# Expert layer: first product as three terms on half-height tiles, rectify and weight in one VectorE step, norm work per tile on ScalarE

## The chip, the cores and the metric

The kernel runs on one core of a Trainium2 chip. The core has a matrix engine (TensorE, PE in the profile), VectorE (DVE), ScalarE (ACT), GpSimd (POOL), and SyncE (SP), which here only issues DMAs. Matrix products land in PSUM, which is eight banks of 512 float32 values in each of 128 partitions; everything else lives in SBUF. The metric is the device time of one execution in microseconds, median of the runs.

## The reference, cut to what matters

Five layers over 8 sequences of 1,024 tokens with 64 features: a token front end, a two-layer recurrence, a routed feed-forward layer, an attention-like layer with phases, and a layer of eight experts. The change is to the last:

```python
gate_logits = x_flat @ Wg + bg + bias
topk_vals, topk_idx = jax.lax.top_k(gate_logits, TOP_K)        # TOP_K = 2 of 8
topk_w = jax.nn.softmax(topk_vals, axis=-1)
combine = (jax.nn.one_hot(topk_idx, NUM_EXPERTS) * topk_w[..., None]).sum(axis=1)
h = jax.nn.relu(jnp.einsum('td,edh->teh', x_flat, W1) + b1)    # D=64 -> 128 hidden, 8 experts
y = jnp.einsum('teh,ehd->ted', h, W2) + b2
out = jnp.einsum('ted,te->td', y, combine)
```

Its input is the layer norm of the running sum `h`, and its output is added to `h`.

## The kernel before

One program, written out by hand for each engine, with semaphores between the engines; nothing is scheduled by a planner. Stages in order: constants and lead-in (to about 45 us), the recurrence (to about 850 us, TensorE without a pause), the routed feed-forward and the phases (to about 905 us), attention (to about 985 us), and the experts (the last 145 us).

**The expert stage** runs over 64 slots, n = 8 b + e for sequence b and expert e. Every slot has this path:

- `hidden(n)` on TensorE (L1667): the first product. The normalised input of a token is kept as two float16 parts, high and low, one above the other in 128 rows of `xt`; the weights `wx[0]` and `wx[1]` (high and low) stand twice above each other. Four matmuls, of 128 rows, 128 columns and 512 tokens, fill two PSUM banks: `bank01` for even slots, `bank45` for odd ones.
- `relu(n)` on ScalarE (L1277): scale, bias and rectify from PSUM to one of eight SBUF buffers, `expert_at(n)`.
- `mult(n)` on VectorE (L2132): multiplies these by `wide[:, e, :]`, the gate weight of expert e for each token, the same in all partitions.
- `second(n)` on TensorE (L1707): the second product in float32, two matmuls of 64 columns each, one for each half of the sequence. In slot e = 0 the products of the gate weights with `eb2` (the second biases, L1718) go ahead of it.

TensorE takes the slots in pairs (L1765): for the pair (n, n + 1) it issues the first products of n + 2 and n + 3, then gate work if it is due, then the second products of n - 1 and n, then transposes. The first product of n + 2 goes into the bank of slot n, so it waits until that has been read: `pe.wait_ge(s_r, n - 1)`, a semaphore that `relu` counts up.

**Beside it, for the next sequences**, each at a fixed slot (`y, step = divmod(n + 3, NE)`):

- The norm of sequence y + 2 (`third_*`): mean, centring, variance, scaling and the low part on VectorE, squares and high part on ScalarE, the root on GpSimd, 8 transposes on TensorE (L321), a copy to `xt` on ScalarE (L327). `mean_back` adds back, on VectorE, a mean that the residual `res` is short of.
- The gates of sequence y + 1: `gates` on TensorE (step 1), `gate_logits` (step 2), `gate_greater` (4), `gate_rank` (5) and `gate_weights` (6) on VectorE, then `weights_turned` on TensorE (step 7: one transpose, L1665, issued behind the two first products of its pair), a copy on ScalarE, a DMA to DRAM and eight DMAs of 512 KB which spread the rows over all partitions (`wide`). SP issues these in order; the one for expert e waits for `mult` of expert e of the sequence before.

Of the kernel before, what the change touches and what calls it, by code (L numbers as in the profile page):

```python
# [15 lines left out]
P = 128  # L16
KEEP = 511
B, T = 8, 1024
D = 64
# [15 lines left out]
W_FF1, W_KQ1, W_V, W_G, W_E1, W_WR, W_END = W_AT = 0, 256, 384, 448, 456, 1480, 1481  # L35
# [5 lines left out]

UNIT = 128
# [48 lines left out]
def build(nc, a, out, kept):  # L91
    with ExitStack() as ctx:
# [11 lines left out]
        M_TURN, M_ALL = bank[7][:, 0:P], bank[7][:, P:P + 8]  # L104
        O_SUM, O_TURN, O_WR = bank[7][:, 0:P], bank[7].bitcast(F16)[:, 2 * P:4 * P], bank[7][:, 2 * P:2 * P + NT]
# [5 lines left out]
        def wide_sums(layer, s):  # L111
# [87 lines left out]
        s_wo, s_sd, s_rs, s_wor, s_wadd = (sem(n) for n in ("att_projected", "att_variance", "att_rstd", "att_scaled",  # L199
                                                            "att_row_added"))  # L200
# [6 lines left out]
        s_hid, s_r, s_gp, s_b2, s_sec, s_moec, s_moet, s_fin = (  # L207
            sem(n) for n in ("expert_hidden", "expert_relu", "expert_weighted", "expert_bias_summed", "expert_summed",
# [7 lines left out]
        ebias = sb("ebias", [P, NE])  # L216
        ffw2 = sb("ffw2", [P, KH, D])
# [19 lines left out]
        def tmp(name, shape, dt=F32):  # L237
# [6 lines left out]
        rest = lo_space[:, W_END:W_END + D]  # L244
        wrec = lo_space[:, 2 * W_END:2 * W_END + 3 * KH * H].rearrange("p (i k h) -> p i k h", i=3, k=KH)
# [37 lines left out]
             (col[:, :], a["col"]), (ebias[:, :], a["ebias"]), (ffw2[:, :, :], a["ffw2"]), (wkq2[:, :], a["wkq2"]),  # L283
# [44 lines left out]


# [278 lines left out]
        wide_at = (0, 256, 384, 448, 456, 712, 968, 1224, 1480, 1481)  # L608
# [19 lines left out]
        def wide_weights(dve, link, c):  # L628
# [6 lines left out]
            else:  # L635
# [3 lines left out]
                if c == 17:  # L639
                    ins.then_inc(s_big, 1)  # L640

# [34 lines left out]
        def rec_tensor(pe, g):  # L676
# [47 lines left out]
            if k == 2 and o == 13:  # L724
                most_turn(pe, most[:, 0:S_END - S_FF1], S_END - S_FF1, 3)
            elif k == 2 and o == 22:
                most_spread(pe, S_END - S_FF1, 3)

# [65 lines left out]
        def rec_vector(dve, link, g):  # L794
# [22 lines left out]
            elif k == 3 and o < 20 and o % 10 != 5:  # L817
                wide_weights(dve, link, o - (o > 5) - (o > 15))

# [70 lines left out]
        xs = tmp("xs", [P, TT, 2, D], F16)  # L890
        whole = tmp("whole", [P, T])
# [33 lines left out]
        last_bank = (bank[3], bank[6])  # L925
        quarters = lambda x, part: x.rearrange("p (h c) -> p h c", h=2)[:, :, part * 256:(part + 1) * 256]
# [166 lines left out]
        def _(act):  # L1093
# [29 lines left out]
            unscale = {i: load_scale(i) for i in (S_FF1, S_KQ1, S_V, S_E1)}  # L1123
# [136 lines left out]

            def third_high(x):
                norm_high(act, B + x, B + x)
# [13 lines left out]

# [999 lines left out]
```

## Time and profile before

| | |
|---|---|
| median of 3 runs | 1132.99 us (1131.59 to 1133.13) |
| the profiled execution | 1132.51 us, of which the span of the instructions is 1130.7 us |
| mean granted TensorE clock | 0.971 of full speed |
| busy over the span | PE 1073.6 us (95%), ACT 771.0 us (68%), DVE 695.6 us (62%), POOL 143.8 us (13%) |
| expert stage | first `mult` starts at 986.80 us, last instruction ends at 1130.7 us |

How to read it: the busy shares are means over stages with different limits. In the expert stage it is the start times of the same instruction in successive sequences that tell the period, and the idle time before an instruction, with the releaser that the profile names, that tells what it waited for. A matmul's duration includes its way through the array; in a row of matmuls the distance from start to start is what one costs.

### The profile page before, as it was taken

How to read it: one execution, taken by the hardware profiler on the slowest of the kernel's cores; microseconds unless marked ns; L12 is line 12 of the kernel's file. 1: busy time of each engine (PE TensorE's matmuls, PEld its weight loads, DVE VectorE, ACT ScalarE, POOL GpSimd, SP SyncE). 2: the span in 40 equal slices, each digit the busy share in tenths (PEclk: the TensorE clock that was granted, in tenths of full speed). 3: DMA queues.
4: the chain of work that ended last, by engine and by line, in shares of the span. 5: the costliest groups of instructions: out<-in, count | busy, mean ns of one | idle time of the engine just before them, and what ended most of it. 6: DMA issues, size and time to landing. Idle time of an engine off the chain costs nothing.

```text
span 1130.7 us, 62476 instructions
## 1 busy us (share of the span) xinstructions
PE 1073.6 (95%) x26880; PEld 870.9 (77%) x26880; DVE 695.6 (62%) x3140; ACT 771.0 (68%) x4577; POOL 143.8 (13%) x220
## 2 busy tenths in 40 slices
PE   4799999999999999999999999999798789999998
PEld 2589899999999999999999999999544388733333
DVE  7566455555555555555555554444457679899995
ACT  1466677777777777777777777766568788656664
POOL 4300000001000110001100010000104202322210
PEclk9599999999999999999999999899799989999999
DMA  5000000000000000000000000000000000346786
GB/s 146 7 10 9 9 9 15 9 10 10 9 14 10 10 9 10 13 10 9 10 5 5 5 4 5 5 4 5 3 1 1 1 2 1 140 164 245 245 287 204
DMA packets 30593, 47.20 MB, mean 42 GB/s; under 512 B 12322, under 2 KB 21611, under 8 KB 30316
## 3 DMA queue, kind: packets, MB, share of 16 engines
q1 hardware_dynamic: 29772, 43.08, 11.4%
q8 instruction: 210, 3.44, 1.2%
q14 instruction: 67, 0.55, 0.2%
q10 hardware_dynamic: 544, 0.13, 0.1%
HBM read 40.84 MB, written 2.36 MB: 38 GB/s over the span
## 4 chain that ended last, share of the span: by engine, by line
PE 86%; DVE 6%; ACT 4%; issue 2%; POOL 1%; DMA 1%; SPq 1%; DVEq 0%; ACTq 0%; POOLq 0%
PE bank L671 44%; PE bank L768 7%; PE bank L1419 6%; PE bank L1724 5%; PE bank L662 5%; PE bank L751 3%; PE bank L432 2%; PE bank L531 2%; PE bank L1452 1%; PE bank L746 1%; PE bank L1601 1%; PE bank L763 1%; DMA bsum<-in_bov 1%; PE bank L321 1%; PE bank L1509 1%
## 5 line engine op out<-in xcount | busy, mean ns | idle before, releaser
L671 PE MATMUL bank<-space,whh_hi 128*128 128x32 f16 (+1 forms) x16384 | 575.7, 175 | 8.4 <-DVE space L799 4.6
L671 PEld LDWEIGHTS bank<-space,whh_hi 128*128 128x128 f16 x16384 | 484.2, 96 | 68.5 <-DVE space L799 8.2
L799 DVE TENSOR_TENSOR space<-h_f,space 128x16 f16<-128x16 f32 x2048 | 287.2, 175 | 361.5 <-ACT h_f L780 356.9
L780 ACT ACTIVATE h_f<-bank 128x16 f32<-128x16 f32 x2048 | 296.2, 184 | 222.9 <-PE bank L671 217.1
L786 ACT ACTIVATE space<-bank 128x16 f16<-128x16 f32 x2048 | 292.3, 184 | 1.1 <-PE bank L671 1.1
L662 PE MATMUL bank<-space,whh_lo 128*128 128x32 f16 (+1 forms) x2096 | 131.2, 177 | 0.0
L768 PE MATMUL bank<-space,wih_hi 128*128 128x32 f16 x2048 | 129.0, 177 | 0.0
L751 PE MATMUL bank<-xr,wih_hi 128*128 128x32 f16 x512 | 97.3, 190 | 0.0
L432 PE MATMUL bank<-onehot,tab 128*128 128x128 f16 x448 | 96.3, 222 | 0.5 <-DVE prepare_cur L482 0.5
L746 PE MATMUL bank<-ones,bias 128*128 128x32 bf16 x512 | 91.6, 179 | 0.0
L662 PEld LDWEIGHTS bank<-space,whh_lo 128*128 128x128 f16 x2096 | 90.0, 96 | 0.0
L1419 PE MATMUL bank<-xt,wx 128*128 128x512 f16 x348 | 87.8, 391 | 2.0 <-ACT xt L327 1.7
L768 PEld LDWEIGHTS bank<-space,wih_hi 128*128 128x128 f16 x2048 | 87.5, 96 | 0.0
L1419 PEld LDWEIGHTS bank<-xt,wx 128*128 128x128 f16 x348 | 31.4, 100 | 56.7 <-issue 16.6
L751 PE MATMUL bank<-xr,wih_lo 128*128 128x32 f16 x512 | 70.6, 193 | 0.0
L352 POOL TENSOR_SCALAR prepare_stat<-prepare_stat 128x2 f32<-128x2 f32 x28 | 6.1, 217 | 478.3 <-DVE prepare_stat L347 478.3
L768 PE MATMUL bank<-space,wih_lo 128*128 128x32 f16 x1024 | 64.4, 176 | 0.0
L763 PE MATMUL bank<-ones,bias 128*128 128x32 bf16 x512 | 52.9, 179 | 0.0
L1281 ACT ACTIVATE space<-bank,ebias 128x1024 f32<-128x1024 f32 x31 | 33.6, 1110 | 26.0 <-PE bank L1419 25.9
L751 PEld LDWEIGHTS bank<-xr,wih_hi 128*128 128x128 f16 x512 | 49.9, 97 | 0.0
L746 PEld LDWEIGHTS bank<-ones,bias 128*128 128x128 bf16 x512 | 49.3, 96 | 0.0
L751 PEld LDWEIGHTS bank<-xr,wih_lo 128*128 128x128 f16 x512 | 45.2, 96 | 0.0
(303 smaller groups left out, 1601.5 us busy)
## 6 DMA issues: line engine op xcount, KB each, us to landing
space<-weights_kept SPq DMA_DIRECT2D x64, 512.0 KB, 7.8
space<-in_x SPq DMA_DIRECT2D x28, 129.0 KB, 3.1
out<-res SPq DMA_DIRECT2D x7, 256.0 KB, 9.8
space<-in_wrec SPq DMA_DIRECT2D x1, 768.0 KB, 4.5
space<-in_wx SPq DMA_DIRECT2D x1, 740.5 KB, 9.0
brec<-in_brec SPq DMA_DIRECT2D x1, 260.0 KB
ew<-in_ew SPq DMA_DIRECT2D x1, 256.0 KB, 4.2
weights_kept<-wturned SPq DMA_DIRECT2D x8, 32.0 KB, 1.8
```

The lines of the kernel that those rows point to most:

```text
L432: mm = pe.matmul(P_CONV[:, b * P:(b + 1) * P], tab[part][:, v, tap, :], onehot[:, m % 2, v, b, tap:tap + P], start=(n == 0), stop=(n == 7) ...
L662: mm = pe.matmul(own[:, m, :], w[:, k, m * P:(m + 1) * P], steps(h, k), start=False, stop=False, skip_group_check=True)
L671: mm = pe.matmul(own[:, m, 0:copies, :], w[:, k, m * P:(m + 1) * P], state[:, k, :].unsqueeze(1).to_broadcast([P, copies, B]), start=False ...
L746: pe.matmul(own, bias[:, m * P:(m + 1) * P], ones[:, 0:U * B], start=(m == 0), stop=False, skip_group_check=True)
L751: pe.matmul(own.rearrange("p s b -> p b s"), (wih0_hi, wih0_lo)[part - 1][:, m * P:(m + 1) * P], xr[:, :, n * U:(n + 1) * U], start=False, ...
L763: pe.matmul(own, bias[:, H + m * P:H + (m + 1) * P], ones[:, 0:U * B], start=(m == 0), stop=False, skip_group_check=True)
L768: pe.matmul(own, w[:, k, m * P:(m + 1) * P], h[0][:, k, at:at + U, part, :], start=False, stop=False, skip_group_check=True)
L780: act.activation(h_f[layer][:, s % 2, :, :], own, ACT.Tanh, scale=scale[layer]).then_inc(s_h[layer], 1)
L786: act.activation(h[layer][:, :, s % RINGS[layer], 0, :], own, ACT.Tanh, scale=scale[layer]).then_inc(s_hi[layer], 1)
L799: dve.tensor_tensor(h[layer][:, :, s % RINGS[layer], 1, :], h_f[layer][:, s % 2, :, :], h[layer][:, :, s % RINGS[layer], 0, :], ALU.subtra ...
L1419: mm = pe.matmul(dst, wx[part][:, w0:w0 + width], xt[:, bass.ds(b * T + half * 512, 512)], start=(part == 0), stop=(part == 1), skip_group ...
L1724: mm = pe.matmul(sum_bank(b)[half * D:(half + 1) * D, :], ew2[:, e, :], expert_at(n)[:, half * 512:(half + 1) * 512], start=False, stop=(e ...
```

## The change

- **First product** (`expert_first`): `third_turn` lays the transposed input out in another way. Of a block of 128 columns, rows 0 to 63 are now tokens of the first half of the sequence and rows 64 to 127 tokens of the second half; the high parts stand in the first 512 columns and the low parts in the other 512. Each half is multiplied on its own 64 rows by the weights there, in three terms (high weights by high input, high by low, low by high), so that a slot has six matmuls of 64 rows, alternating between the halves and between two banks, where it had four of 128 rows.
- **`relu` is gone.** `mult` reads PSUM itself, and does `max(sum, -b1) * weight` in one `scalar_tensor_tensor`. What this leaves out, `b1` times the weight through the second product, is put into the second biases: eight small matmuls against a diagonal of `b1` (`ediag`) and three VectorE steps, in the recurrence, make `eb2_scaled`. The bank of slot n is now free when `mult` has read it: TensorE waits for `s_gp` where it waited for `s_r`.
- **Norm of sequences 3 to 7** in the expert stage: centring, squares (with the sum taken by the same instruction) and `mean_back` are done by ScalarE, one instruction per tile of 128 tokens, 8 for each; VectorE keeps the mean, the scaling and the low part.
- **Gates**: 12 matmuls of 16 columns where there were 16 of 8, with `Wg` in a block form.

```diff
-                    pe.wait_ge(s_r, n - 1)
+                    pe.wait_ge(s_gp, n - 1)
...
+            def expert_first(n, own, at, count):
+                b, e = divmod(n, NE)
+                for c, (w, part) in enumerate(PARTS):
+                    for half in range(2):
+                        rows = slice(half * D, half * D + D)
+                        mm = pe.matmul(own[:, half * 512 + at:half * 512 + at + count],
+                                       wx[w][rows, W_E1 + e * HE:W_E1 + (e + 1) * HE],
+                                       xt[rows, bass.ds(b * T + part * 512 + at, count)],
+                                       start=(c == 0), stop=(c == 2), skip_group_check=True)
...
             def mult(n):
-                dve.wait_ge(s_r, n + 1)
+                dve.wait_ge(s_hid, n + 1)
+                if n >= 8:
+                    dve.wait_ge(s_sec, n - 7)
                 dve.wait_ge(s_wide_row[e], 16 * (b + 1))
-                dve.tensor_tensor(own, own, wide[:, e, :], ALU.mult).then_inc(s_gp, 1)
+                dve.scalar_tensor_tensor(expert_at(n), banks[n % 2 * 2][:, :], ebias[:, e:e + 1], wide[:, e, :], ALU.max,
+                                         ALU.mult).then_inc(s_gp, 1)
...
             def last_hidden(part):
-                pe.wait_ge(s_r, n - 1)
+                pe.wait_ge(s_gp, last - 1 + part)
...
+            def third_centre(x):
+                act.wait_ge(s_sum3, x - 2)
+                act.wait_ge(s_nrm, B + x)
+                for t in range(TT):
+                    ins = act.activation(xc[:, t, :], res[:, x * TT + t, 0:D], ACT.Identity, bias=stat[:, 0, t:t + 1],
+                                         scale=-float(D))
+            def mean_back(x):
+                for t in range(TT):
+                    own = res[:, x * TT + t, :]
+                    ins = act.activation(own[:, 0:D], own[:, 0:D], ACT.Identity, bias=own[:, D:D + 1])
...
+            elif k == 3 and o < NE:
+                mm = pe.matmul(E_BIAS, ediag[:, o, :], ew2[:, o, :], start=(o == 0), stop=(o == NE - 1),
+                               skip_group_check=True)
```

What stands in a row on the engines, at three places. Bank names are pairs: `bank01` holds even slots, `bank45` odd ones; `eye,gleft` is the transpose of the gate weights.

TensorE, the pair of slots 8b + 4 and 8b + 5 (second half of a sequence). Before:

```order
L1419 MATMUL bank45<-xt,wx0 128x512 [waits expert_relu]
L1419 MATMUL bank45<-xt,wx1 128x512
L1419 MATMUL bank45<-xt,wx0 128x512
L1419 MATMUL bank45<-xt,wx1 128x512
L1665 MATMUL bank67<-eye,gleft 64x128 [waits weights_ready_for_turn]
L1724 MATMUL bank67<-gp,ew2 64x512 [waits expert_weighted]
L1724 MATMUL bank67<-gp,ew2 64x512
```

After:

```order
L1724 MATMUL bank45<-xt,wx0 128x512 [waits expert_weighted]
L1724 MATMUL bank45<-xt,wx0 128x512 x3
L1724 MATMUL bank45<-xt,wx1 128x512 x2
L1716 MATMUL bank67<-eye,gleft 64x128 [waits weights_ready_for_turn]
L1778 MATMUL bank67<-gp,ew2 64x512 [waits expert_weighted]
L1778 MATMUL bank67<-gp,ew2 64x512
```

The rows keep their places. The product ahead of the gate transpose waited for `relu`, and waits now for `mult`, of slot 8b + 5.

VectorE, slots 8b + 4 to 8b + 7 and the logits of the next sequence. Before:

```order
L2137 TENSOR_TENSOR space<-space 128x1024 [waits weights_of_expert4_loaded,expert_relu]
L315 TENSOR_TENSOR xs<-nrmw,xs 128x8x64 [waits norm_high]
L2142 TENSOR_TENSOR res<-bank23,res 128x8x64 [waits experts_turned]
L2137 TENSOR_TENSOR space<-space 128x1024 [waits weights_of_expert5_loaded,expert_relu]
L2032 TENSOR_REDUCE stat<-res 128x8
L2137 TENSOR_TENSOR space<-space 128x1024 [waits weights_of_expert6_loaded,expert_relu,dve_order]
L2036 SCALAR_TENSOR_TENSOR xc2<-stat,res 128x8x64 [waits normalised]
L2137 TENSOR_TENSOR space<-space 128x1024 [waits weights_of_expert7_loaded,expert_relu]
L2060 SCALAR_TENSOR_TENSOR lg<-bank67,inv,gate_bias 128x64 [waits gates_compared,gates_summed]
```

After:

```order
L2196 SCALAR_TENSOR_TENSOR space<-bank01,ebias,space 128x1024 [waits weights_of_expert4_loaded,expert_summed,expert_hidden]
L2112 TENSOR_TENSOR xs<-nrmw,xs 128x2x4x64 [waits norm_high]
L2203 TENSOR_TENSOR res<-bank23,res 128x8x64 [waits mean_back,experts_turned]
L2196 SCALAR_TENSOR_TENSOR space<-bank45,ebias,space 128x1024 [waits weights_of_expert5_loaded,expert_summed,expert_hidden]
L2090 TENSOR_REDUCE stat<-res 128x8 [waits centred]
L2196 SCALAR_TENSOR_TENSOR space<-bank01,ebias,space 128x1024 [waits weights_of_expert6_loaded,expert_summed,expert_hidden]
L2196 SCALAR_TENSOR_TENSOR space<-bank45,ebias,space 128x1024 [waits weights_of_expert7_loaded,expert_summed,expert_hidden]
L2118 SCALAR_TENSOR_TENSOR lg<-bank67,inv,gate_bias 128x64 [waits gates_compared,gates_summed]
```

Centring (L2036) has left; nothing stands between the last `mult` and the logits, and every `mult` reads PSUM.

ScalarE, from the copy of the transposed gate weights to the high part of the next norm. Before:

```order
L1275 ACTIVATE wturned<-bank67 64x128 [waits weights_in_dram,weights_turned]
L1281 ACTIVATE space<-bank45,ebias 128x1024 [waits expert_summed,expert_hidden]
L327 ACTIVATE xt<-bank23 128x1024 [waits norm_turned]
L1281 ACTIVATE gel<-bank01,ebias 128x1024 [waits expert_summed,expert_hidden]
L1259 ACTIVATE sq<-xc2 128x512 [waits centred]
L1281 ACTIVATE gel<-bank45,ebias 128x1024 [waits expert_summed,expert_hidden]
L1281 ACTIVATE gp<-bank01,ebias 128x1024 [waits expert_summed,expert_hidden]
L1269 ACTIVATE gex<-gc 128x64 [waits gates_shifted]
L1281 ACTIVATE gp<-bank45,ebias 128x1024 [waits expert_summed,expert_hidden]
L1303 ACTIVATE yt<-bank67 128x512 [waits experts_turned,expert_summed]
```

After:

```order
L1333 ACTIVATE wturned<-bank67 64x128 [waits weights_in_dram,weights_turned]
L330 ACTIVATE xt<-bank23 128x1024 [waits norm_turned]
L1300 ACTIVATE xc2<-res,stat 128x64 [waits normalised,third_summed]
L1300 ACTIVATE xc2<-res,stat 128x64 x7
L1307 ACTIVATE sq,stat<-xc2 128x64 [waits centred]
L1307 ACTIVATE sq,stat<-xc2 128x64 x7
L1327 ACTIVATE gex<-gc 128x64 [waits gates_shifted]
L1314 ACTIVATE res<-res 128x64 x8
L1346 ACTIVATE yt<-bank23 128x512 [waits experts_turned,expert_summed]
L1320 ACTIVATE xs<-nrmw 128x2x4x64 [waits norm_turned,normalised]
```

The four `relu` rows have left and 24 rows of one tile each have come.

## Rows read from the trace of the kernel before

**Rows 1.** Chain of waits, expert stage: start us, us, what and how many records.

```profile
1020.59 1.73 PE bank L1419 x8
...
1022.70 1.87 PE bank L1724 x8
...
1027.40 1.00 PE bank L1718 x4
```

**Rows 2.** Waits of the expert stage: us in total, times, longest us.

```profile
ACT space L1281 <- PE bank L1419: 25.9, 15, 2.2
...
DVE gel L2137 <- DMA space<-weights_kept: 4.8, 3, 3.5
```

**Rows 3.** VectorE in order of time: start us, us, engine, line, operation, out<-in.

```profile
1006.75 0.28 DVE L2060 SCALAR_TENSOR_TENSOR lg<-bank,inv,gate_bias 128x64 f32<-128x64 f32 x1
...
1008.15 1.21 DVE L2137 TENSOR_TENSOR gel<-gel,space 128x1024 f32<-128x1024 f32 x1
...
1046.21 0.68 DVE L2069 TENSOR_TENSOR gdiff<-gdiff,order 128x512 f32<-128x512 f32 x1
1046.92 0.69 DVE L2041 SCALAR_TENSOR_TENSOR res<-res 128x512 f32<-128x512 f32 x1
...
1048.79 0.68 DVE L2073 TENSOR_REDUCE grank<-gdiff 128x64 f32<-128x512 f32 x1
...
1049.73 0.69 DVE L2051 TENSOR_TENSOR nrmw<-xc,stat 128x512 f32<-128x512 f32 x1
1050.34 1.22 DVE L2137 TENSOR_TENSOR gp<-gp,space 128x1024 f32<-128x1024 f32 x1
1051.48 0.22 DVE L2078 TENSOR_TENSOR gc<-gex,gsel 128x64 f32<-128x64 f32 x1
...
1052.36 1.22 DVE L2137 TENSOR_TENSOR space<-space 128x1024 f32<-128x1024 f32 x1
1053.50 0.68 DVE L315 TENSOR_TENSOR xs<-nrmw,xs 128x512 f16<-128x512 f32 x1
1054.10 0.68 DVE L2142 TENSOR_TENSOR res<-bank,res 128x512 f32<-128x512 f32 x1
```

**Rows 4.** Order of time: transpose of the gate weights, and VectorE's first multiplications behind it.

```profile
1087.62 0.27 PE L1665 MATMUL bank<-eye,gleft 128*64 128x128 f32 x1
...
1095.42 1.22 DVE L2137 TENSOR_TENSOR gel<-gel,space 128x1024 f32<-128x1024 f32 x1 [0.89 <-DMA space<-weights_kept]
1097.10 1.23 DVE L2137 TENSOR_TENSOR gel<-gel,space 128x1024 f32<-128x1024 f32 x1 [0.45 <-DMA space<-weights_kept]
...
1105.10 0.27 PE L1665 MATMUL bank<-eye,gleft 128*64 128x128 f32 x1
...
1111.80 1.23 DVE L2137 TENSOR_TENSOR gel<-gel,space 128x1024 f32<-128x1024 f32 x1 [3.51 <-DMA space<-weights_kept]
...
1114.13 1.23 DVE L2137 TENSOR_TENSOR gel<-gel,space 128x1024 f32<-128x1024 f32 x1 [1.10 <-ACT gp L1281]
```

**Rows 5.** TensorE in order of time: one full product, two half-column products, the last one.

```profile
873.08 1.10 PE L1509 MATMUL bank<-gel,wkq 128*128 128x512 f32 x2
...
1028.34 1.08 PE L1724 MATMUL bank<-gel,ew 128*64 128x512 f32 x4
...
1125.23 1.03 PE L1697 MATMUL bank<-space,ew 128*64 128x256 f32 x8
```

**Rows 6.** Busy time by stretch: us, PE, PEld, DVE, ACT, POOL, granted clock, DMA.

```profile
994.00:996.00 2.00, 0.03 (x2) 0.00 (x0) 1.93 (x4) 0.31 (x1) 0.89 (x1) 1.00 0.00 0
...
998.00:1000.00 2.00, 2.00 (x6) 0.73 (x5) 1.93 (x5) 1.56 (x2) 0.00 (x0) 0.50 0.00 0
```

**Rows 7.** Chain of waits, attention: float32 matmuls with 64 moving columns, two records each.

```profile
974.43 1.51 PE bank L1611 x14
```

**Rows 8.** Groups by line, expert stage: small ScalarE instruction, root on GpSimd; busy us, mean ns, idle.

```profile
L1070 POOL TENSOR_TENSOR stat<-stat,nhalf 128x8 f32<-128x8 f32 x8 | 15.4, 1927 | 0.7
...
L1269 ACT ACTIVATE gex<-gc 128x64 f32<-128x64 f32 x8 | 2.0, 247 | 0.0
```

More of the change, by code:

```diff
@@ L327, in norm_copy, with third_turn @@
             act.activation(dst, src.bitcast(F16)[:, 0:T], ACT.Copy).then_inc(s_xt, 1)
+        def third_turn(pe, dst, x):
+            pe.wait_ge(s_xs, OPEN + B + x + 1)
+            pe.wait_ge(s_xt, OPEN + B + x)
+            for part in range(2):
+                for i in range(4):
+                    at = (part * 4 + i) * P
+                    mm = pe.transpose(dst.bitcast(F16)[:, at:at + P],
+                                      xs3[:, part, i, :, :].rearrange("p h d -> p (h d)"), eye16[:, :])
+            mm.then_inc(s_tr, 1)
         def mean_of(dve, link, r, total):
@@ L890, in build @@
         xs = tmp("xs", [P, TT, 2, D], F16)
+        xs3 = xs[:, :, :, :].rearrange("p t a d -> p (t a d)").rearrange("p (a i h d) -> p a i h d", a=2, i=4, h=2)
+        xs3_by = [xs3[:, part, :, :, :].rearrange("p i h d -> p h i d") for part in range(2)]
+        by_half = lambda x: x.rearrange("p (h i) d -> p h i d", h=2)
         whole = tmp("whole", [P, T])
@@ L1336, in _ @@
                 y, step = divmod(n + 3, NE)
-                if n + 1 < last:
-                    relu(n + 1)
-                elif n + 1 == last:
-                    last_relu(0)
-                    last_relu(1)
                 if step == 0 and y < B:
@@ L1345, in _ @@
                     third_copy(y + 1, bank[3])
+                if step == 1 and y + 2 < B:
+                    third_centre(y + 2)
                 elif step == 2 and y + 2 < B:
-                    third_square(y + 2)
+                    third_squares(y + 2)
                 elif step == 4 and y + 1 < B:
                     gate_exp(y + 1)
+                elif step == 5 and y + 2 < B:
+                    mean_back(y + 2)
                 elif step == 7 and y + 2 < B:
                     third_high(y + 2)
+                if n in (0, 1):
+                    mean_back(n)
                 if e == 2 and b:
@@ L1660, in gates @@
                     pe.wait_ge(s_wgt_c, x)
-                on_norm_tokens(dst, W_G, NE, x).then_inc(s_gt, 1)
+                for i in range(4):
+                    for c, (w, part) in enumerate(PARTS):
+                        mm = pe.matmul(dst.rearrange("p (h i e) -> p h i e", h=2, i=4)[:, :, i, :],
+                                       xt[:, bass.ds(x * T + part * 512 + i * P, P)], wx[w][:, W_G:W_G + 2 * NE],
+                                       start=(c == 0), stop=(c == 2), skip_group_check=True)
+                mm.then_inc(s_gt, 1)
             def weights_turned(x, dst):
@@ L2037, in third_centre @@
                                          ALU.add).then_inc(s_xc, 1)
-            def mean_back(x):
-                own = res[:, span(x), :]
-                link(dve.scalar_tensor_tensor(own[:, :, 0:D], spread(own[:, :, D]), 1.0 / D, own[:, :, 0:D], ALU.mult,
-                                              ALU.add))
             def third_variance(x):
@@ L2223, in lay_out @@
     eb2[:NE] = f("L1_ffn_b2")
+    ediag = z(P, NE, NE)
+    for i in range(NE):
+        ediag[:, i, i] = f("L1_ffn_b1")[i]
     p = np.arange(P)
```

139 lines of the change are left out of this document (78 added, 61 removed).

## The prediction

> **What bounds the kernel now.** I read three views of the last 145 us. The chain of waits first: from 1003 to 1126 us it is made of nothing but TensorE pieces, one behind the other, such as two slots' first products in 1.73 us, two slots' second products in 1.87 us, the bias products in 1.00 us [rows 1]. The waits say the same from the other side: `relu` waited for first products, 25.9 us in one of its three groups [rows 2]. Then VectorE in order of time, which gives its steps from start to start: a multiplication takes 1.14 us (1050.34 to 1051.48), `gate_greater` 0.71, `gate_rank` 0.94, the scaling 0.61, `gate_weights` 0.88, low part 0.60, the addition of the experts about 0.6, the logits 1.40 (1006.75 to 1008.15) [rows 3]. VectorE has hardly a gap, so TensorE bounds, and VectorE is close behind. Last the hand-over of the gate weights: from the transpose on TensorE to the first multiplication with them went 6.70 us (1105.10 to 1111.80) and 7.80 us (1087.62 to 1095.42), both ended by the DMA, and the second multiplication followed 2.33 and 1.68 us after the first, where 1.14 is its own time [rows 4]. (The profile puts the 1.10 us before 1114.13 down to ScalarE, on a tile that this step does not read; I take it as the DMA of the second row.) From 1008.15 to 1111.80 are six sequences: 17.3 us each [rows 3, 4]. The waits name the DMA ahead of three multiplications only [rows 2], so in the other sequences the weights were there in time.
>
> **What each part costs, taken alone.** All against the profiled execution: 1132.5 us, 0.5 below the median of the three runs.
>
> First product: six matmuls instead of four. If the two halves run side by side, three rounds at 1.73/8 = 0.216 us are 0.65 us a slot, 0.22 less than now; if not, 1.30 us, 0.43 more. No row has products on separate rows. The nearest is separate columns: four records of the second product, in two halves, take 1.08 us, and one product over the full array with as many tokens 1.10 us in two records [rows 5], so column halves do run side by side. I take 0.65, and keep 1.30 as a rival. The page "TensorEngine Tiling (Array Packing)" of the Trainium skill, section Key Properties, says that different tiles load and multiply in parallel; rows 5 agree for columns, and no row here shows it for rows.
>
> Multiplication: `relu` leaves ScalarE, and the fused step costs VectorE 1.14 us as before: the addition that reads PSUM took 0.68 us and a step of the same size out of SBUF 0.69 [rows 3]. The page "VectorE: DVE Perf Modes" of the Trainium skill, section The TRN2 errata, counts 120 cycles of fixed cost with a PSUM source against 58 from SBUF, which at 0.96 GHz would be an estimated 0.06 us more per slot, 4 us over 64. The trace does not agree at 512 elements, and the row decides.
>
> VectorE loses centring, variance and `mean_back`, three steps like the 0.69 us of `mean_back` [rows 3], about 2 us a sequence; its own steps then sum to 8 x 1.14 + 0.71 + 0.94 + 0.61 + 0.88 + 0.60 + 0.60 + 0.7 (mean) + 1.40 = 15.5 us a sequence. ScalarE gets 24 small instructions of 0.25 us [rows 8] or some more, 6 to 8 us, in place of eight `relu`. They lie beside other work: the mean of the next norm ends near 14 us in the walk below, its copy of `xt`, centring and squares near 22, the root on GpSimd (1.93 us and an addition, about 3 together [rows 8]) near 25, and the scaling that needs it comes near 26.6. That cover is thin: 1.5 us.
>
> The bias work in the recurrence adds eight float32 matmuls of 64 columns to steps where TensorE never pauses. Seven such take 1.51 us in attention, 0.22 each [rows 7]; with only 8 weight columns some less. Between 0.9 and 1.8 us; I take 1.2.
>
> **The wait that is added.** This decides. The first product of slot n + 2 now waits for the multiplication of slot n, and behind it in TensorE's queue stand the gate transpose, the gates, and two second products. VectorE is in order too, with 6.4 us of other steps a sequence between its multiplications. So I walk through one sequence from the start of its first multiplication, at 0, with the second at 2.0 (mean of 2.33 and 1.68):
>
> VectorE: `gate_greater` 3.1, third multiplication 3.8, rank 5.0, scaling 5.9, fourth multiplication 6.5, weights 7.7, fifth 8.5, low part 9.7, ready to add at 10.3. TensorE: the product for the fourth multiplication starts when the second ends, 3.2 to 3.9; then second products with the biases (2 x 0.93 + 1.00 = 2.9) to 6.8; product 7.4; the next product waits for the fourth multiplication (7.7), to 8.4; second products 1.9, to 10.3; transposes of the sum, 0.6, to 10.9. The addition waits for these until 11.0, so the sixth multiplication starts at 11.6 and ends at 12.8. Only now can the product ahead of the gate transpose run, to 13.5, and the transpose starts at 13.5. With 7.2 us of hand-over (the mean of 6.70 and 7.80) the next sequence starts at 20.7 us. That is 3.4 more than 17.3, in six sequences: **+20.4 us**. In the sequence before them, 21.35 us long (986.80 to 1008.15), the two engines wait for each other already; by the same steps its transpose comes a little later, and I take +0.3, an estimate between -1 and +1.5.
>
> The last sequence has no gates, but from its first multiplication the same loop runs: product 3.9, second products and biases 6.8, two products 8.1, second products and sum transposes 10.6, addition 11.3, sixth multiplication to 12.5, seventh to 13.7, the last half product 14.1, four slots' second products 17.8, the last halves 18.7. Before, from 1111.80 to the end of the last product at 1126.26, it was 14.5 [rows 4, 5]. **+4.1 us.**
>
> **Clock.** TensorE now idles around each sequence's start: about 2.4 us before the first product behind it and 1.3 before the second. In the trace a pause of 2.1 us (994 to 996) was followed by a granted clock of 0.50 at 998 to 1000 [rows 6], that is 1.2 GHz for 2.4. At half clock the product and second products after 3.2 us above would take up to 1.7 us more, with the same delay on the addition and the transpose. Over seven sequences 0 to 12 us; the one row gives about 3.6 us at half clock, of which some 1.1 us of extra time would fall on the path, and I take it in every third sequence: +2.6.
>
> Sum: 20.4 + 0.3 + 4.1 + 1.2 + 2.6 = 28.6, on 1132.5: **1161 us**.
>
> **Rivals.**
>
> *The weights come in time, and the logits' loop bounds.* Without the hand-over, the sixth multiplication ends at 12.0; product 12.8, gate transpose 13.0, second products 14.8, norm transposes 15.4, two products 16.7, gates 17.2, logits from 17.3 to 18.7, next sequence. It is 1.4 us over 17.3 in five sequences (7), about 1 us less in the first and the one without later gates (-2), +4.1 at the end, +1.2: 1143 us. For it: in most sequences of before nothing waited for the DMA [rows 2]. Against: none of the two measured hand-overs was under 6.70 us, and it takes 5.7.
>
> *The halves do not run side by side.* A product is then 1.30 us. Three of them lie on the path of each sequence and two in the last: period 22.9 instead of 20.7, and +17 us in all: 1178 us. Against it the column halves in rows 5; for it, no row on rows.
>
> *Faster: VectorE's own sum becomes the bound.* If first products always stood ready and the weights came in time, 15.5 us a sequence, 1.8 less in seven: 1132.5 - 12.6 + 1.2 = 1121 us. It decides at the transpose: from 12.8 in the walk, the hand-over and product would have to fit into 17.3 - 12.8 = 4.5 us for even no change, and they take 7.9. Also a variant in which gains and waits cancel, near 1133, is possible where ScalarE's and TensorE's steps slide into other gaps than I see.
>
> **How the numbers follow.** The forecast's mechanism (hand-over on the path, with more or less half clock) 0.66; logits' loop alone 0.12; halves one after the other 0.12; not slower 0.10, of which 0.07 faster and 0.03 within 0.2%, about what a measurement of this kernel tells from no change. The costs' bounds: with 7.8 and 2.33 in the hand-over the period is 21.6, +5.6 us; with 6.7 and 1.68, -5; half clock everywhere +9.4. So the mechanism alone spans 1150 to 1177. Taking in the two slower rivals, the range is 1143 to 1179. Faster 0.07, same 0.03, slower 0.90.
>
> **What would show it.** Distance between the first multiplications of two sequences: 20 to 22 us, ended by a DMA wait of 1 to 2 us before the first and about 1 before the second. Before the logits a wait of VectorE for the gates of 1 to 3 us. TensorE waiting for the multiplication (`expert_weighted`) ahead of the first products, over 3 us a sequence, and a granted clock under 1.00 in the stage. Two slots' first products in 1.3 us show halves side by side; 2.6 us show the rival. The recurrence may be longer by 1 to 2 us and no more. I am wrong if the period is under 17.3 us, if VectorE shows no idle time before the multiplications, or if something outside the expert stage moves by more than 3 us.

## The result

The changed kernel took 1172.77 us (median of 4 runs, 1165.02 to 1180.47) against 1132.29 us for the kernel before (4 runs, 1131.12 to 1133.13): a ratio of 1.0356, with a 95% interval of 1.0325 to 1.0387. It is slower by 40 us. The profiled execution took 1170.27 us, with a span of 1168.5 us. Its runs also differ more: 15 us from the fastest to the slowest, where the kernel before has 2, and the longer ones have the lower mean granted clock (1165.02 us at 0.962, 1180.47 us at 0.945).

VectorE's first multiplication of the expert stage starts at 986.94 us, before it was 986.80. So on balance nothing is lost ahead of the stage, and 37.7 of the 37.8 us of span are lost in it. These are the stretches from one sequence's first multiplication to the next one's. Columns: us, busy time of PE, PEld, DVE, ACT and POOL (with records), granted clock, DMA share, GB/s. First the kernel before, three of its eight:

```profile
1043.34:1060.83 17.49, 17.45 (x99) 6.41 (x97) 17.15 (x27) 11.45 (x15) 4.13 (x4) 1.00 0.75 267
...
1095.42:1111.80 16.38, 16.38 (x74) 5.38 (x73) 12.21 (x16) 9.25 (x11) 0.00 (x0) 1.00 0.79 272
1111.80:1130.70 18.90, 15.09 (x77) 5.61 (x75) 11.14 (x12) 7.66 (x10) 0.00 (x0) 0.99 0.63 217
```

and the changed kernel, all eight:

```profile
986.94:1009.76 22.82, 17.87 (x101) 5.19 (x101) 18.09 (x25) 12.25 (x56) 5.21 (x5) 0.85 0.38 132
1009.76:1031.82 22.06, 17.86 (x109) 5.40 (x109) 16.17 (x22) 7.78 (x34) 2.95 (x3) 0.92 0.52 191
1031.82:1052.55 20.73, 16.61 (x111) 5.15 (x109) 16.03 (x23) 8.53 (x38) 2.94 (x3) 1.00 0.62 221
1052.55:1072.65 20.10, 16.63 (x111) 5.16 (x109) 16.03 (x22) 8.60 (x39) 2.95 (x3) 1.00 0.63 223
1072.65:1097.36 24.71, 19.64 (x109) 5.67 (x109) 16.17 (x22) 8.87 (x42) 2.94 (x3) 0.86 0.56 189
1097.36:1117.21 19.85, 16.58 (x109) 5.16 (x109) 15.42 (x21) 5.76 (x22) 2.95 (x3) 1.00 0.65 222
1117.21:1141.71 24.50, 18.69 (x89) 4.86 (x89) 12.96 (x17) 0.87 (x2) 0.00 (x0) 0.86 0.52 183
1141.71:1168.50 26.79, 17.46 (x94) 5.32 (x94) 11.60 (x12) 1.25 (x3) 0.00 (x0) 0.85 0.46 159
```

Read the second table twice. No engine is busy all the time any more: at full clock TensorE works 16.6 of 20.1 us and VectorE 16.0, where before TensorE worked 17.45 of 17.49. And among the six sequences between the first and the last there are two kinds: 19.9 to 20.7 us where the clock column says 1.00, and 24.5 or 24.7 where it says 0.86; one, of 22.06 us at 0.92, lies between them.

VectorE's waits show what a sequence now consists of; in brackets stands the idle time ahead of an instruction and what ended it:

```profile
1070.77 0.28 DVE L2118 SCALAR_TENSOR_TENSOR lg<-bank,inv,gate_bias 128x64 f32<-128x64 f32 x1 [2.39 <-PE bank L1709]
...
1072.65 1.28 DVE L2196 SCALAR_TENSOR_TENSOR gel<-bank,ebias,space 128x1024 f32<-128x1024 f32 x1 [0.40 <-PE bank L1778]
1075.55 1.28 DVE L2196 SCALAR_TENSOR_TENSOR gel<-bank,ebias,space 128x1024 f32<-128x1024 f32 x1 [1.61 <-DMA space<-weights_kept]
```

The logits wait 2.39 us for the gates, the second multiplication 1.61 us for its row of gate weights. (The profile puts the 0.40 us before 1072.65 down to second products that this multiplication does not wait for by the program; I take them as the DMA of the first row.) On TensorE, the first products wait for the multiplication ("PE bank L1724 <- DVE gel L2196: 26.7, 16, 3.1" in the waits, with 9.5 more for the other buffers). The chain of waits goes straight through the hand-over, columns start and length:

```profile
1110.05 0.82 PE bank L1724 x6
1110.87 0.24 PE bank L1716
1111.14 0.28 ACT wturned L1333
1111.43 1.77 DMA weights_kept<-wturned
...
1113.97 5.66 DMA space<-weights_kept
```

First product, gate transpose, copy, store, load: 9.3 us from the transpose (1110.80) to the second multiplication (1120.10). Loads and stores of these weights hold 52% of the chain between 1090 and 1120 us; from 1003 to 1126 us of the kernel before it was made of TensorE alone [rows 1].

### The profile page after: what moved, and what is told of

The parts are those of the page before. It is cut to its first block, busy times and chain, and to the rows that moved or that the text cites. A ratio compares the mean times of both kernels' runs of the same rounds, so it can differ in the third digit from the quotient of the medians.

```text
span 1168.5 us, 62781 instructions
## 1 busy us (share of the span) xinstructions
PE 1077.4 (92%) x26994; PEld 861.8 (74%) x26994; DVE 688.4 (59%) x3124; ACT 736.6 (63%) x4707; POOL 137.0 (12%) x220
## 4 chain that ended last, share of the span: by engine, by line
PE 79%; DVE 8%; DMA 5%; ACT 4%; issue 2%; POOL 1%; SPq 1%; DVEq 0%; ACTq 0%; POOLq 0%
PE bank L695 42%; PE bank L797 7%; PE bank L686 4%; DMA space<-weights_kept 4%; PE bank L780 3%; PE bank L1778 3%; PE bank L445 2%; PE bank L544 2%; PE bank L1724 2%; PE bank L1465 1%; PE bank L1498 1%; PE bank L775 1%; DMA weights_kept<-wturned 1%; PE bank L1647 1%; PE bank L792 1%
## 5 line engine op out<-in xcount | busy, mean ns | idle before, releaser
L1724 PE MATMUL bank<-xt,wx 64*128 64x512 f16 (+1 forms) x390 | 55.8, 407 | 36.3 <-DVE gel L2196 26.7
L1724 PEld LDWEIGHTS bank<-xt,wx 64*128 64x128 f16 x390 | 15.7, 99 | 77.9 <-DVE gel L2196 37.7
L2196 DVE SCALAR_TENSOR_TENSOR space<-bank,ebias,space 128x1024 f32<-128x1024 f32 x31 | 38.8, 1277 | 9.1 <-PE bank L1724 9.1
```

The lines of the kernel that those rows point to most:

```text
L1724: mm = pe.matmul(own[:, half * 512 + at:half * 512 + at + count], wx[w][rows, W_E1 + e * HE:W_E1 + (e + 1) * HE], xt[rows, bass.ds(b * T + ...
L2196: dve.scalar_tensor_tensor(expert_at(n), banks[n % 2 * 2][:, :], ebias[:, e:e + 1], wide[:, e, :], ALU.max, ALU.mult).then_inc(s_gp, 1)
```

## The experiments

Theory 1 is that of the prediction: a first product that waits for VectorE's multiplication puts the gate transpose late, and the transfer behind it on the path. Rivals: the loop of gates and logits bounds (2), the half clock is a loss of its own (3), the new product or ScalarE's tile work costs (4).

The ratios are to runs of the kernel before that were taken beside each run; their medians lie between 1132.29 and 1133.29 us. `e5_product_only` and `e6_relu_mean_early` have 10 runs each, the others 4.

| run | median us | ratio to before, 95% interval |
|---|---|---|
| changed kernel | 1172.77 | 1.0325 to 1.0387 |
| e1_turn_early | 1146.79 | 1.0104 to 1.0164 |
| e2_logits_late | 1180.20 | 1.0379 to 1.0462 |
| e3_both_moved | 1146.57 | 1.0098 to 1.0174 |
| e4_relu_back | 1144.58 | 1.0077 to 1.0111 |
| e5_product_only | 1130.64 | 0.9970 to 0.9989 |
| e6_relu_mean_early | 1131.27 | 0.9975 to 1.0000 |
| e7_norm_back | 1177.19 | 1.0378 to 1.0425 |
| e8_no_spread | 1145.67 | 1.0097 to 1.0130 |
| e9_filler | 1164.11 | 1.0257 to 1.0291 |
| e10_squares | 1126.63 | 0.9929 to 0.9962 |
| e11_squares_middle | 1125.51 | 0.9923 to 0.9956 |

### The transpose earlier, the logits later

```diff
                 pair = (2 * k, 2 * k + 1)
+                for n in pair:
+                    y, step = divmod(n + 3, NE)
+                    if step == 7 and y + 1 < B:
+                        weights_turned(y + 1, ...)      # no longer behind the two products
                 for n in pair:
                     if n + 2 < last:
                         hidden(n + 2)
```

> Edit: TensorE transposes the gate weights ahead of the two first products of its pair of slots, instead of behind them. Nothing else moves. Theory 1 (the chain of the prediction: multiplication, first product, gate transpose, 6 to 8 us of hand-over, next sequence): the transpose comes some 2.5 us earlier, and the sequence becomes shorter by that until the logits' loop bounds at about 19 us; 10 to 16 us less than the changed kernel, 1155 to 1163 us, and fewer microseconds ended by the DMA. Theory 2 (the loop over the gates and logits bounds already): the transpose had time to spare, and the time stays within 3 us of 1172. Theory 3 (the half clock is the main loss, and the pauses that bring it are elsewhere): the periods keep two lengths, about 20 and 24.6 us.

Measured: 1146.79 us, 26 us less. The transpose comes 10.3 us behind the sequence's first multiplication (1057.99 behind 1047.70) instead of 13.7 (1066.21 behind 1052.55), VectorE's multiplications wait for the weights twice in the whole stage (2.9 us) instead of 12 times (15.6 us), and the six middle sequences all run at full clock: 19.35 us, four times 18.91 or 18.92, and 17.14. Two of them:

```profile
1047.70:1066.61 18.91, 16.46 (x111) 5.13 (x109) 15.84 (x23) 8.50 (x39) 2.95 (x3) 1.00 0.70 244
1066.61:1085.52 18.91, 16.46 (x111) 5.13 (x109) 15.85 (x23) 8.50 (x39) 2.94 (x3) 1.00 0.72 242
```

Theory 2 falls, since moving the transpose alone could gain nothing by it. Its 18.7 us for the logits' loop is what is late next: 18.91. The gain is larger than the 10 to 16 us expected because the sequences of 24.6 us are gone too: about 11 of the 26 us are half clock (the excess over 20.2 us in the table above), the rest is the shorter period and the end of the stage. That no second length is left, though only the transpose moved, speaks against theory 3 as a cause by itself.

```diff
-                    if step == 2:
+                    if step == 3 and n:
                         gate_logits(y + 1, bank[6][:, 0:TT * NE])
```

> Edit: VectorE takes the next sequence's logits one slot later, behind the multiplication of slot 0 instead of slot 7. Theory 1 (the hand-over of gate weights bounds): VectorE no longer waits 2.4 to 3.0 us for the gates, but then waits for the weights' DMA instead; between no gain and 4 us. Theory 2 (the logits' loop bounds): 1.4 us or more in each of five or six sequences, 8 to 15 us less than 1172. Behind the multiplication of slot 0 stands the comparison on GpSimd, which now starts later, so gate_greater may wait: a loss of up to 1 us a sequence is possible under both.

Measured: 1180.20 us (1175.90 to 1185.83), 7 us above the changed kernel, whose four runs reach to 1180.47. Theory 2 falls again, and theory 1 had named no loss but that of a waiting `gate_greater`, which does not show: nothing waits ahead of it. The trace shows this:

```profile
1059.37 1.28 DVE L2196 SCALAR_TENSOR_TENSOR gel<-bank,ebias,space 128x1024 f32<-128x1024 f32 x1 [4.46 <-DMA space<-weights_kept]
1060.57 0.27 DVE L2118 SCALAR_TENSOR_TENSOR lg<-bank,inv,gate_bias 128x64 f32<-128x64 f32 x1
...
1081.92 1.28 DVE L2196 SCALAR_TENSOR_TENSOR gel<-bank,ebias,space 128x1024 f32<-128x1024 f32 x1 [4.44 <-DMA space<-weights_kept]
```

The logits' 1.4 us had stood in the shadow of the transfer. Now they stand behind the first multiplication, between two steps of the chain. In the two sequences at full clock (21.22 and 21.32 us, where the changed kernel has a mean of 20.2) the transpose comes 14.59 us behind the first multiplication (1052.74 behind 1038.15, 1096.51 behind 1081.92) instead of 13.44 to 14.40; in the one shown above it is 16.0 us (1075.32), but there half clock has its part (0.92). So the move costs about 1.0 us a sequence, some 6 of the 7 us. Theory 1 was right on where the bound lies, and I had not followed it to its end: of what left the shadow of the transfer for the chain, most of the length came back as a loss.

> Edit: both the earlier gate transpose and the later logits. Theory 1: with the hand-over earlier by 2.5 us and the logits no longer ahead of slot 0, the sequence falls to 17.5 to 18.5 us, and TensorE's pauses get shorter, so the clock stays up: 1138 to 1152 us, more than the sum of the two gains of the single edits. Theory 3 (the clock): nearly the same as the earlier transpose alone, the periods still alternate with the granted clock.

Measured: 1146.57 us (1143.41 to 1154.07), in the range, but no better than the transpose alone. By the letter it is more than the sum of the two single changes, since the later logits alone lost 7 us and beside the earlier transpose lose nothing. Four middle sequences are shorter, 17.97 to 18.30 us; the first is 19.40 at a clock of 0.91, and the one ahead of the last is 18.88 instead of 17.14. A gain over the earlier transpose isn't shown.

### The transfer taken away

Sequences 2 to 8 are weighted with the first sequence's gates.

```diff
-                    if x:
-                        sp.wait_ge(s_gp, NE * (x - 1) + e + 1)
-                    sp.dma_start(wide[:, e, :], ...)
+                    if x == 0:
+                        sp.dma_start(wide[:, e, :], ...)
```

> Edit, to the changed kernel: the spread rows of gate weights are loaded for the first sequence alone and used for all, so no multiplication waits for the DMA behind the gate transpose. The output is not the reference's: sequences 2 to 8 are weighted with the first sequence's gates. The transpose, its copy and the stores stay. Theory 1: the part of the chain behind the transpose is gone, and the logits' loop bounds at 18.7 to 19.2 us, nearly without pauses long enough for the clock to fall: 1143 to 1155 us, close to the run with the earlier transpose. Theory 2 (logits' loop bounds already in the changed kernel): under 5 us less than 1172. Theory 3 (the clock by itself): the two lengths of 20 and 24.6 us stay.

Measured: 1145.67 us (1145.42 to 1146.02), five middle sequences of 19.13 to 19.15 us and a sixth of 15.91, all at a clock of 1.00. So the transfer of the gate weights, with the clock that goes with its pauses, is worth 27 us. It agrees with the run with the earlier transpose, in which the transfer was not taken away but started 3.4 us earlier. What is left, 19.14, is the coupling itself with the logits' loop.

### The clock

```diff
                 for n in pair:
+                    if n >= NE and n % NE < 2:
+                        for i in range(6 + 2 * (n % NE)):
+                            pe.matmul(bank[7], wx[0][:, W_E1:W_E1 + P], wx[0][:, W_E1:W_E1 + 512], ...)
                     if n + 2 < last:
                         hidden(n + 2)
```

> Edit, to the changed kernel: TensorE gets 6 products of 128 x 512 on the weights, whose result nobody reads, ahead of the first product that waits for a sequence's first multiplication, and 8 ahead of the one that waits for its second, 1.3 and 1.7 us of work in pauses of 1.4 and 2.1 us. The work for the result, and every wait, stay. Theory 1 with the clock as its echo (the pauses make the sequence 20 us long, and the half clock behind them makes some of them 4.6 us longer): the granted clock stays at 1.00, all middle sequences are 19.9 to 20.7 us, and the time is 10 to 16 us less, 1156 to 1163 us, with a smaller spread from run to run. Rival (the half clock falls where TensorE has slack, and costs little): within 3 us of 1172, though the clock is up. If the filling delays the products that it stands in front of, up to 0.3 us a time, 4 us in all come back.

One thing in this was wrong: bank 7 holds the sums of every second sequence, so their result is read and the output is not the reference's. No wait is changed by it. Measured: 1164.11 us (1163.47 to 1165.33), 1 us above the range of theory 1. The two kinds of sequence are gone:

```profile
1033.62:1054.81 21.19, 19.88 (x125) 6.46 (x124) 16.03 (x23) 8.70 (x41) 2.94 (x3) 1.00 0.65 218
1054.81:1075.66 20.85, 19.35 (x123) 6.35 (x122) 16.03 (x22) 8.28 (x37) 2.95 (x3) 1.00 0.59 212
```

Work that does nothing made the kernel 8.7 us faster, and the runs agree within 2 us instead of 15. The sequences are 20.9 to 21.8 us instead of 20.2, so the filling itself costs about 1 us each (0.7 to 1.6). The clock is therefore worth more than 8.7 us; the changed kernel's own table gives 24.71, 24.50 and 22.06 against a mean of 20.2 at full clock, 10.7 us, and some 2.6 in the last sequence (26.79 against 24.17 in this run). With a clock that stays up the changed kernel would, by an estimate from these 13.3 us and the measured 8.7, still be 27 to 32 us slower than before. Here is such a stretch, TensorE in order of time in the changed kernel:

```profile
1073.99 0.82 PE L1724 MATMUL bank<-xt,wx 64*128 64x512 f16 x6 [1.40 <-DVE gel L2196]
1076.89 0.82 PE L1724 MATMUL bank<-xt,wx 64*128 64x512 f16 x6 [2.07 <-DVE gel L2196]
1077.64 1.35 PE L1778 MATMUL bank<-space,ew 128*64 128x512 f32 x4
1078.91 1.97 PE L1772 MATMUL bank<-whole,eb_scaled 8*64 8x512 f32 x4
1080.82 1.98 PE L1778 MATMUL bank<-gel,ew 128*64 128x512 f32 x4
1082.72 2.65 PE L1724 MATMUL bank<-xt,wx 64*128 64x512 f16 x12
1085.30 1.08 PE L1778 MATMUL bank<-gel,ew 128*64 128x512 f32 x4
```

Behind the pauses of 1.40 and 2.07 us everything takes about twice its time (1.97 us where it takes 1.07, 2.65 where it takes 1.47) for 7 us. This is the granted clock at 1.2 instead of 2.4 GHz (0.50 from 1080 to 1084 us), and the second products, on which the addition waits, are in it.

### The parts of the change one by one

```diff
             def mult(n):
-                dve.wait_ge(s_hid, n + 1)
-                dve.scalar_tensor_tensor(expert_at(n), banks[n % 2 * 2][:, :], ebias[:, e:e + 1], wide[:, e, :], ALU.max,
-                                         ALU.mult).then_inc(s_gp, 1)
+                dve.wait_ge(s_r, n + 1)
+                dve.tensor_tensor(own, own, wide[:, e, :], ALU.mult).then_inc(s_gp, 1)
...
-                    pe.wait_ge(s_gp, n - 1)
+                    pe.wait_ge(s_r, n - 1)
```

> Edit: ScalarE rectifies again, the multiplication works in SBUF, the bank is free for the next first product after the rectification, and the bias is not scaled by the gate; the first product in three terms on 64 rows and the norm's tile work on ScalarE stay. Theory 1 (the coupling of TensorE to VectorE's multiplication is the cause): the pauses are gone. TensorE has 0.22 us a slot less than in the kernel before, and VectorE about 2 us a sequence less, so it is faster than the kernel before: 16 to 17 us a sequence, 1118 to 1130 us, TensorE at full clock. Theory 4 (the first product in three terms, or the norm on ScalarE, is what costs): it stays above 1150 us.

Measured: 1144.58 us, between the two expectations. The coupling is gone and 28 us with it, but it is not the kernel that I expected. TensorE's pause, in order of time:

```profile
1048.15 0.82 PE L1737 MATMUL bank<-xt,wx 64*128 64x512 f16 x6 [0.36 <-ACT gel L1332]
1051.06 1.46 PE L1737 MATMUL bank<-xt,wx 64*128 64x512 f16 x6 [2.09 <-ACT gel L1332]
```

and what ScalarE did ahead of it and in it:

```profile
1045.09 2.00 ACT L1293 ACTIVATE xc<-res,stat 128x64 f32<-128x64 f32 x8
1047.00 1.09 ACT L1332 ACTIVATE gel<-bank,ebias 128x1024 f32<-128x1024 f32 x1
1047.99 0.24 ACT L1300 ACTIVATE sq<-xc 128x64 f32<-128x64 f32 x1
...
1049.90 1.10 ACT L1332 ACTIVATE gel<-bank,ebias 128x1024 f32<-128x1024 f32 x1
```

Eight centrings (2.00 us) stand ahead of one rectification and eight squares with the reads of their sums (1.9 us, from 1047.99 to 1049.90) ahead of the next, and TensorE waits 2.09 us for a bank. The granted clock falls around this pause: four of the middle sequences were 20.1 to 21.9 us at 0.84 to 0.92, and the one ahead of them, with the same pause of 2.09 us, 18.49 us at 1.00. In the changed kernel the same steps lie beside other work, since nothing on ScalarE releases a bank there. So the two parts of the change, moving the norm to ScalarE and taking the rectification from it, go together, and the next two runs put the norm back on VectorE, the first with rectification on ScalarE, the second without:

> Edit: as the run with rectification back on ScalarE, and centring, variance and mean_back are VectorE's again as before the change; only the first product in three terms on 64 rows, with its layout of the tokens, is left of the change. Theory 1b (read from the run before it: ScalarE's 8 centrings and 8 squares, 3.9 us in one piece, stand ahead of the rectifications and so ahead of TensorE's banks): the sequence falls from 20 us to what VectorE's own steps take, 17.1 to 17.5 us, and the time is 1129 to 1135, about the kernel before. Theory 4b (the product's own form costs, by its 64-row weight loads or its clock): it stays at 1140 us or above.

> Edit, to the changed kernel: centring, variance and mean_back are VectorE's again; the fused multiplication that frees the bank, the scaled biases and the first product stay. Theory 1 (multiplication, first product, transpose and hand-over make the sequence): every VectorE step between two multiplications lengthens the chain, so 0.7 to 1.4 us a sequence more, 1174 to 1190 us, with the spread that the clock brings. Theory 4 (the norm's small steps on ScalarE cost in the changed kernel, as they do where ScalarE rectifies): it becomes faster, under 1165 us.

Product alone: 1130.64 us, 0.2% faster than before (interval 0.1 to 0.3%), with three of the middle sequences at 17.48 us. TensorE is busy 16.52 of them, VectorE 17.14:

```profile
1043.42:1060.90 17.48, 16.52 (x111) 5.13 (x109) 17.14 (x26) 11.44 (x15) 4.13 (x3) 1.00 0.79 258
```

The product in three terms saves TensorE 0.22 us a slot, as it should (two slots' products take 1.40 us from start to start, 1046.46 to 1047.86, where they took 1.84), its busy time in a sequence falls by 0.9, and the kernel hardly moves, since VectorE bounds at the same length. The changed kernel with its norm on VectorE: 1177.19 us, not faster; sequences at full clock are 21.1 to 22.2 us, and 20.34 the sixth, instead of 19.9 to 20.7. Theory 4 falls on both sides: neither the product nor ScalarE's tile work is the loss in the changed kernel.

### Towards a faster kernel

> Edit: as the run that keeps of the change the first product alone, but mean_back stays on ScalarE (8 small steps, 2.0 us) and the gate transpose is issued ahead of its pair's first products. Theory 1b: VectorE has 0.69 us a sequence less, so 16.4 to 16.9 us a sequence where ScalarE's 2.0 us don't hold up a rectification; 1120 to 1130 us, faster than the kernel before. If ScalarE's piece of 2.0 us does hold up a first product, as its piece of 3.9 us did, it is 1 us a sequence worse instead: 1132 to 1142 us.

Measured: 1131.27 us. Middle sequences are 16.8 to 17.3 us but for one of 18.36; the transpose now waits 0.69 to 1.95 us for `gate_weights` in six sequences (1.95 ahead of 1085.79, in the one of 18.36 us). It ended between the two ranges that were expected, and settles neither.

Back to the product alone, with squares and `mean_back` on ScalarE in pieces of four:

```diff
-                if step == 2 and y + 2 < B:
-                    third_square(y + 2)
+                if step in (2, 3) and y + 2 < B:
+                    third_squares(y + 2, step - 2)      # tiles 0 to 3, 4 to 7
...
+                elif step in (5, 6) and y + 2 < B:
+                    mean_back(y + 2, range(4 * (step - 5), 4 * (step - 4)))
```

> Edit, to the run that keeps of the change the first product alone: squares with their sums (8 small steps, in two slots of 4) and mean_back (8, in two slots of 4) go to ScalarE, centring stays on VectorE. Theory 1b (a long piece on ScalarE holds up rectifications; VectorE's own steps bound otherwise): with pieces of 1 us nothing is held up, VectorE has 1.4 us a sequence less, TensorE's 15.6 to 16.5 us bounds, and the sequence is 16.2 to 16.8 us: 1121 to 1127 us. If any ScalarE work ahead of a rectification lands on the path, whatever its length, it stays at 1130 us or above.

> Edit, to the run before it: the transpose of the gate weights is issued between the two first products of its pair, 0.7 us earlier. If a sequence's first multiplication still ended in a wait for the DMA, this takes up to 0.7 us of it away in each of six sequences: 1118 to 1125 us. If TensorE then waits for gate_weights of VectorE, which bound the run with the transpose ahead of both (0.69 to 1.16 us a time), it gains nothing: within 1.5 us of the run before it.

Measured: 1126.63 and 1125.51 us, 0.6% faster than the kernel before. The second has this in the middle of the stage:

```profile
1041.46:1057.64 16.18, 16.18 (x113) 5.25 (x111) 15.87 (x24) 14.48 (x39) 4.15 (x3) 1.00 0.78 266
```

TensorE is busy for the whole of it. ScalarE works 14.5 of 16.2 us and delays nothing there, with 16 small steps a sequence where the first run with rectification had 24 and was 18 us slower; here no piece is longer than four of them, about 1 us. The second run was to be within 1.5 us of the first if nothing was gained, and it is 1.1 us less. Whether the earlier transpose helps is open: the two intervals overlap almost wholly.

## Why the prediction was right, and where not

**The walk was right.** It put the gate transpose 13.5 us behind the first multiplication; at full clock it was 14.40 (1046.22 behind 1031.82), 13.66 (1066.21 behind 1052.55) and 13.44 (1110.80 behind 1097.36). It gave a period of 20.7 us; at full clock it was 20.73, 20.10 and 19.85. Six sequences at their mean of 20.2 are 121.4 us against 103.7 before (17.49 + 17.70 + 17.49 + 17.47 + 17.12 + 16.38), so the +20.4 of the sum was +17.7. The hand-over was shorter than its 7.2 us, 6.33 to 6.81 to the first multiplication (6.44 and 6.41 behind the transposes at 1066.21 and 1110.80), and behind these two the second came 2.90 and 2.89 us later, not 2.0: the same end of the transfer in all. Elsewhere it came 1.3 to 2.5 us later. The waits of the first multiplication were 0.3 to 0.9 us, and 5.03 in the last sequence, those of the second up to 2.3; the logits waited 2.4 to 3.0 us where 1 to 3 were expected.

**The clock was mis-sized.** "In every third sequence", 1.1 us each, +2.6 in all. It fell in two of the six wholly and in one partly (24.71, 24.50, 22.06), and a hit cost 4.3 to 4.5 us, not 1.1: the slow stretch lasted 7 us and not the 3.6 that the one row gave, and it covers the second products on which the addition and the fifth multiplication wait. With the last sequence the term was 13 us instead of 2.6, a little over the 12 that I had set as its bound. This is more than the whole distance from 1161 to 1170.3: the period, 2.7 us too long in the sum, ran against it. So the sum came as close as it did partly by luck, while the mechanism is what the runs show.

**The first and the last sequence.** First: +1.5 (22.82 against 21.35), expected +0.3, the upper end of its estimate, at a clock of 0.85. Last: +7.9 (26.79 against 18.90), expected +4.1; 2.6 of it is the clock just counted. Its second multiplication came 3.58 us behind the first (1141.71, 1145.29) where the walk had 2.0, and its products up to 1149.9 ran at half clock.

**The recurrence's term held, but does not show in the total.** +1.2 was expected, and the expert stage starts only 0.1 us later (986.94 against 986.80). The bias products are there, 16 records of 219 ns on TensorE between 82.8 and 89.5 us, and each of the eight steps of the recurrence that they stand in is longer. The first of them:

```profile
82.07 0.56 PE L695 MATMUL bank<-space,whh_hi 128*128 128x32 f16 x16
...
82.79 0.28 PE L753 MATMUL bank<-ew,ediag 128*8 128x64 f32 x2
83.00 0.56 PE L695 MATMUL bank<-space,whh_hi 128*128 128x32 f16 x16
```

It takes 0.93 us; the steps before take 0.74, and so does the same step of the kernel before. All eight take 0.93 to 0.97 us, together 1.7 us more. In this execution the recurrence began 1.3 us earlier (34.2 us against 35.5) and the stages behind it were 1.1 us shorter, which hides it.

**The multiplication.** Taken at 1.14 us, it was 1.20 from start to start. In the changed kernel it takes this long:

```profile
L2196 DVE SCALAR_TENSOR_TENSOR space<-bank,ebias,space 128x1024 f32<-128x1024 f32 x31 | 38.8, 1277 | 9.1 <-PE bank L1724 9.1
```

Before, each was 1.21 to 1.23 us [rows 3, 4]. The row that I let decide, an addition of 512 elements, did not carry over to another operation. It is not the number of elements: the fused step of the last slot, with 512 elements from PSUM, took 0.75 us, while the addition from PSUM and a `scalar_tensor_tensor` out of SBUF, of 512 elements each, took 0.69. The Trainium skill, page "VectorE: DVE Perf Modes", section The TRN2 errata, had the higher fixed cost of a PSUM source, by which I had an estimate of 0.06 us; the measured rise of 0.06 agrees with it, though source and operation changed together and the addition shows no such cost. In the 5 multiplications that lie on a sequence's chain it is 0.3 us, within the period that was measured.

**The halves do run side by side.** Two slots' first products, 12 matmuls, take 1.40 us from start to start (1068.87 to 1070.27) where 1.3 were forecast and 2.6 was the rival; before, 8 matmuls took 1.84 (1046.74 to 1048.58). One sum of mine was off: three products of 0.65 us more on the path make a period of 22.65 us, not the rival's 22.9. The rival of the logits' loop is the kernel that one gets once the transpose is early: 18.9 us, where its walk had 18.7.

## What to carry to other kernels

Before two engines are joined by fusing a step, walk the chain from the buffer that the fused step frees to the next transfer that depends on it, and ask what the in-order queue puts between: here the two slots' products ahead of a small transpose cost 26 us, half clock included, and issuing the transpose ahead of them gave these back. Work that costs nothing in the shadow of a transfer can cost most of its length once it is moved into the chain (1.0 of 1.4 us here), and small steps on an engine that frees buffers should come in pieces shorter than that engine's slack. Where an engine that is no longer the bound starts to pause, price the lower clock behind the pauses over all the work that follows and not over the step behind the gap.

## What the runs showed of the hardware

- In the changed kernel TensorE pauses twice at each sequence's start, a product apart. Pauses of 1.40 and 2.07 us, and of 1.38 and 2.06, were followed by 7 us at half clock, 1.88 and 1.63 by 3 to 4 us; 1.29 and 0.83 (ahead of 1055.54), 1.27 and 1.56 (ahead of 1035.55), 1.77 and 0.45 (ahead of 1099.97) were not. The lengths of the pauses alone do not tell the cases apart: with the later logits 1.59 and 1.76 us (ahead of 1063.29) were followed by 3 to 4 us at half clock, and 1.57 and 1.76 (ahead of 1085.85) and 1.77 and 1.76 (ahead of 1042.08) by none; with rectification back on ScalarE the pause of 2.09 us was followed by none once (ahead of 1010.45), once by 7 us (ahead of 1029.13), and three times half clock lasted 3 to 4 us around it. So one program can fall on either side, which would explain runs that differ by 15 us (argued, not tried apart from the filling). Products in the pauses kept the clock at 1.00 in all middle sequences.
- Six matmuls of 64 rows and 512 columns in fp16, in pairs on the two row halves, take 0.70 us in a row of pieces, half of what six on the full array would need by the kernel before (8 in 1.84 us, 0.23 each).
- A square of 64 columns with its sum on ScalarE is two records, 0.24 and 0.19 us; eight take 1.9 us.
